# The products of the quantised x with its block scales, walked elements-first instead of blocks-first

## What is computed

```python
def fp4_quant_dequant(x):
    xb = x.reshape(shape[:-1] + (shape[-1] // BLOCK, BLOCK))      # BLOCK = 16
    scale = jnp.max(jnp.abs(xb), axis=-1, keepdims=True) / 6.0
    scale = jnp.maximum(scale, jnp.float32(1e-12))
    xn = xb / scale
    idx = jnp.searchsorted(_MID, jnp.abs(xn))
    q = _GRID[idx] * jnp.sign(xn) * scale
    return q.reshape(shape)
...
gate = fp4_linear(x, w_gate); y = fp4_linear(x, w_up)             # 256 -> 704
h = jax.nn.silu(gate) * y
return fp4_linear(h, w_down)                                      # 704 -> 256
...
x = x + 0.5 * ffn(layernorm(x))
x = x + attn(layernorm(x))     # scan over 512 tokens, 16 states per channel
x = x + 0.5 * ffn(layernorm(x))
```

## Time and profile before

| what | value |
|---|---|
| median of 3 runs | 3746.4 us (3733.61 to 3751.59) |
| the profiled execution's own time | 3731.64 us |
| its span | 3729.6 us |
| VectorE busy | 3399.4 us, 91% |
| TensorE busy (matmul) | 3292.7 us, 88% |
| ScalarE busy | 2999.9 us, 80% |
| GpSimd busy | 2873.4 us, 77% |
| granted TensorE clock, mean | 0.966 |
| DMA queue of SP | 24.3% of 16 engines' span |

### The profile page before, as it was taken

One profiled execution on the slowest core, in us unless ns is written; L12 is line 12 of the kernel. 1 busy time (PEld: TensorE's weight loads), 2 busy tenths in 40 slices (PEclk: granted clock), 3 DMA queues, 4 the chain that ended last, 5 costly groups with the idle time before them and its releaser, 6 DMA issues. The chain is left out here.

```text
span 3729.6 us, 79626 instructions
## 1 busy us (share of the span) xinstructions
PE 3292.7 (88%) x28716; PEld 2351.3 (63%) x28716; DVE 3399.4 (91%) x5419; ACT 2999.9 (80%) x6314; POOL 2873.4 (77%) x2489
## 2 busy tenths in 40 slices
PE   0589999999998999999999999999999999999984
PEld 0256666666666666666666666666666666666663
DVE  5499999999999999999999999999999999999984
ACT  1388888888888888888888888888888888888872
POOL 2458788788877788787878878788888888888854
PEclk9799999999999999999999999999999999999987
DMA  2112222222222222222222222222222222232212
GB/s 37 25 33 49 52 52 54 58 60 46 59 49 51 54 63 47 55 55 49 55 58 61 45 59 49 54 53 60 50 55 60 49 55 54 58 63 43 53 35 43
DMA packets 583023, 192.07 MB, mean 51 GB/s; under 512 B 544039, under 2 KB 578280, under 8 KB 582632
## 3 DMA queue, kind: packets, MB, share of 16 engines
q1 hardware_dynamic: 582632, 186.98, 24.3%
HBM read 19.16 MB, written 16.78 MB: 10 GB/s over the span
## 5 line engine op out<-in xcount | busy, mean ns | idle before, releaser
L787 DVE TENSOR_TENSOR_SCAN state<-w_ps,decay 128x512 f32<-128x512 f32 x1024 | 1210.6, 1208 | 60.3 <-PE w_ps L1303 56.5
L1229 PE MATMUL gu_ps<-wgu,qxT 128*128 128x352 f16 x6144 | 1032.6, 320 | 101.9 <-ACT gate L1048 51.4
L1303 PE MATMUL w_ps<-bdif,x_parts 128*128 128x129 f16 (+1 forms) x12288 | 850.3, 222 | 96.0 <-DVE state L787 88.5
L1303 PEld LDWEIGHTS w_ps<-bdif,x_parts 128*128 128x128 f16 x12288 | 754.0, 98 | 218.4 <-issue 175.3
L1229 PEld LDWEIGHTS gu_ps<-wgu,qxT 128*128 128x128 f16 x6144 | 577.1, 99 | 480.7 <-ACT gate L1048 65.3
L1115 ACT ACTIVATE decay<-dt,A_sb 128x512 f32<-128x512 f32 x1024 | 686.3, 711 | 71.0 <-DVE state L787 43.6
L797 DVE SCALAR_TENSOR_TENSOR c_state<-state,inv_A,rep_ps 128x512 f32<-128x512 f32 x1024 | 723.1, 738 | 7.7 <-issue 3.5
L495 POOL TENSOR_TENSOR bdif<-dif,B_lo 128x516 f16<-128x516 f16 x512 | 535.9, 1060 | 164.7 <-PE w_ps L1303 164.0
L1243 PE MATMUL dn_ps<-wd,qhT 128*128 128x256 f16 (+1 forms) x4608 | 591.6, 279 | 64.0 <-DMA qhT<-qh 62.5
L1323 PE MATMUL y_ps<-ident,c_state 128*128 128x128 f32 x4352 | 621.5, 279 | 22.7 <-DVE c_state L797 22.7
L1103 ACT ACTIVATE bdif<-dif,B_tok 128x129 f16<-128x129 f16 x2048 | 628.9, 393 | 0.0
(11 more groups left out here) (160 smaller groups left out, 3803.3 us busy)
## 6 DMA issues: line engine op xcount, KB each, us to landing
x_in<-in_L_attn_x SPq DMA_DIRECT2D x32, 512.0 KB, 3.8
x_s<-x_a SPq DMA_DIRECT2D x32, 512.0 KB, 3.8
out<-x_out SPq DMA_DIRECT2D x32, 512.0 KB, 3.2
qhT<-qh SPq DMA_TRANSPOSE x256, 3.7
qxT<-qx SPq DMA_TRANSPOSE x128, 3.1
hid<-in_L_ffn_w_gate SPq DMA_DIRECT2D x1, 704.0 KB
bdif<-in_L_ffn_w_up SPq DMA_DIRECT2D x1, 704.0 KB
val<-in_L_ffn_w_down SPq DMA_DIRECT2D x1, 704.0 KB, 13.1
```

The costliest lines, as they stand in the source:

```text
L787: v.tensor_tensor_scan(state[:, n % 2, gi, :], w_ps[:, gi, :], decay[:, n % 2, gi, :], 0.0, ALU.add, ALU.mult).then_inc(state_ready.sem, 1)
L1229: last = te.matmul(gu_ps[:, m, 0:FH], qxT[:, t // 2, 4 * (t % 2) + xp * G + c], wgu[:, c, wp, a:a + FH], start=begin, stop=end)
L1303: last = te.matmul(w_ps[:, gi, t * P:t * P + wide], x_parts[:, seq % 2, xp, t, gi * P:(gi + 1) * P], bdif[:, n % NB, t, bp, 0:wide], start ...
```

## The change

`parts_x` describes the same elements in another order. x_grid and qx keep their layout in memory (position outer, block inner); the instruction now walks them as [tile, block, position], the position innermost. Both x_grid and qx are then stepped by 16 elements (32 bytes) from one element to the next, and each scale is read 16 times in a row. Number of instructions, their sizes, their types, their waits, and the place in every engine's order are the same.

```diff
-            def by_position(t, nb):
-                return t.rearrange("p (t i b) -> p t i b", i=BLOCK, b=nb)
-
-            def over_positions(t, nb, groups):
-                r = t.rearrange("p (t b) -> p t b", b=nb).unsqueeze(2)
-                return r.broadcast_to([t.shape[0], groups, BLOCK, nb])
+            def over_blocks(t, nb, groups):
+                r = t.rearrange("p (t b) -> p t b", b=nb).unsqueeze(3)
+                return r.broadcast_to([t.shape[0], groups, nb, BLOCK])
...
                 for part, s in ((0, x_scale_hi), (1, x_scale_lo)):
-                    v.tensor_tensor(qx[:, a:b, part, :].rearrange("p t (i b) -> p t i b", b=XB_),
-                                    by_position(x_grid[:, a * DM:b * DM], XB_),
-                                    over_positions(s[:, a * XB_:b * XB_], XB_, TH),
+                    v.tensor_tensor(qx[:, a:b, part, :].rearrange("p t (i b) -> p t b i", b=XB_),
+                                    x_grid[:, a * DM:b * DM].rearrange("p (t i b) -> p t b i", i=BLOCK, b=XB_),
+                                    over_blocks(s[:, a * XB_:b * XB_], XB_, TH),
                                     ALU.mult).then_inc(qx_ready.sem, 1)
```

## The result

The changed kernel takes 4209.2 us in the median (4207.2 to 4211.4, 4 runs), the kernel before beside it 3740.0 us. The ratio is 1.129 (95% interval 1.124 to 1.134): 12.9% slower, 483 us by the ratio, where I had forecast 3910 us and a range up to 3995. The direction was right; the size was 2.7 times the 179 us of my sum.

What follows compares the result with a forecast made beforehand. VectorE was taken to bound the kernel. 256 products at 0.757 us more each add 194 us, 15 hide: 3731.6 + 194 - 15 = 3911, forecast as 3910 us (chance 0.60), range 3790 to 3995.

Steps and rivals of the forecast that it cites:

- What bounds the kernel: VectorE is the fullest engine, 94.7% busy in the steady stretch, against TensorE at 93% and POOL at 81%.
- First price, the half rate: Each of the 256 changed products loses its packed rate: 688 ns in place of 415, 273 ns more.
- Second price, the step: 32-byte steps in each changed product: 323 ns for the write, 161 for the read, giving 1172 ns in all.
- The page's figures: Skill page, 32-bit streams: 1.71 ns a column for a hopping write, 1.98 with both reads too; product about 1.17 us.
- Rival 2: The step costs more, up to 1.5 us a product: 278 us less 20, kernel at 3989 us; chance 0.15.
- rival 1: Changed products at half rate with no price for the step: 70 us less 5, kernel at 3797 us; chance 0.12.
- rival 5: Loop order is turned back on the way to the chip, nothing changes: 3732 us; chance 0.03.
- rival 3: The 194 us replace half of VectorE's idle time, 90 us hidden in its waits: 3836 us; chance 0.07.
- Rival 4: Not slower: at N.qy0, POOL stalls (34 us) and 30 us of waits go, at half rate alone: 3738 us; chance 0.03.
- What hides: Only N.qy1's extra 1.5 us, in VectorE's wait for TensorE at the head of ten iterations: 15 us.
- The transpose of N.qy0: Starts 1.5 us later, covered by 2.4 us before TensorE's first gate and up product; no cost.
- The cost beside it, POOL: VectorE's products and POOL exclude each other: 34 us of stalls stay; holding POOL longer costs nothing, 10 us at range top.

Runs made afterwards that it cites:

- e1: Kernel before, with only the scale read 16 times in a row, x_grid and qx both in order: 3786.7 us, ratio 1.015.
- e3: Kernel before, with the scale read 16 times in a row and x_grid's read stepped by 32 bytes, qx in order: 3955.2 us, ratio 1.062.
- e2: Kernel before, with the scale read 16 times in a row and qx's write stepped by 32 bytes, x_grid in order: 4207.2 us, ratio 1.129.

## Why the prediction was wrong, point by point

- **What bounds the kernel: right.** VectorE's busy time rose by 491 us, its idle time fell from 330 to 316 us, and the span grew by 477. Three doses say the same: busy time of the group up by 57, 200 and 545 us in e1, e3 and e2 gave 56, 229 and 480 us by the ratios (in e2 the products overlap as above, so that VectorE's busy time rose by 491 and not 545).
- **First price, the half rate: right.** 684 ns measured in e1 against 688 in the sum, from L724 and the 4-byte rows.
- **Second price, the step: this is the step that failed.** I took "L944, in full for the write, and with half of it again for the read", 484 ns, and let the bounds end at 1500 ns for the product. The write alone costs 1668 ns over e1 where the sum had 323, and the read adds nothing to it where the sum had 161. L944 was a fair witness for its own kind: 4-byte elements pay 1.05 to 1.08 us here too. But the changed write has elements of 2 bytes, and no row of the trace wrote such an element by itself; I noted the smaller size only as a reason for a lower price. The upper bound was built from reads and writes of 4-byte elements and so could not hold it. Adding a share for the read was wrong as well: the two sides do not add in any of the steps tried.
- **The page's figures**, "Vector Engine (DVE) Microarchitecture Reference" of the Trainium skill, section 5.2, led to the same 1.17 us, because they are for 32-bit streams. Where these runs have 32-bit streams, with one read and the write hopping, they come out lower than its 1.98 ns a column for both reads and the write: (1.07 - 0.69)/512 + 1.03 = 1.77 ns, no more than the write alone.
- **Rival 2 had the right sign of the error and the wrong size.** In place of its 278 us the group of products grew by 544, and VectorE's busy time by 491. Rivals 1 and 5 are out by the product's duration, rival 3 by the idle time, which fell by 14 us and not by 90. Rival 4 is out by e1, which has its condition, the half rate alone: it took 62 us more than the kernel before (56 by the ratio), near the 65 of rival 1's sum, and not the 6 of rival 4's.
- **What hides: near in size, partly by luck.** I let 15 us vanish; idle time fell by 14. The waits at the head of an iteration shrank as I had said, from 56.5 us to 29.9 for L784, and none is over 2.7 us, where ten were over 3. But those 27 us are not all of it: the waits of `hid` for TensorE grew by 16 us (65.7 to 81.6) and for ScalarE by 8. And e3, whose product is the nearest to my 1172 ns (1081 and 1075), hid nothing: VectorE's idle time grew by 17 us, its wait at the same place from 56.5 to 90.7, and the stalls beside POOL from 34 to (169 + 334) x 128 = 64. It lost 229 us where my sum with its product would have 256 x 0.66 - 15 = 154. So with the product's price right, the sum would still have been some 75 us short there. Why the waits grew there and shrank in the changed kernel was not tried.

```profile
DVE state L784 <- PE w_ps L1300: 90.7, 34, 3.8
```

- **The transpose of N.qy0: covered, as forecast.** At 2041 us its two products end 5.96 us after the first one's start, against 3.29 at 1930.4. TensorE still waits for it only twice, 30.8 us where it was 21.5, since TensorE is late by the same delay: it waits 235 us for c_state at L1310 and 155 at L1320, where it waited 14 and 23 before:

```profile
PE rep_ps L1310 <- DVE c_state L794: 235.3, 69, 8.5
PE y_ps L1320 <- DVE c_state L794: 154.5, 30, 7.2
```

- **The cost beside it, POOL: a little short.** The stalls, which I had left as they were, rose from 34 to (137 + 302) x 128 = 56 us, and POOL in turn is held: its L484 takes 3.36 us at 2041 us and its next L495 2.66, where they took 2.13 and 1.23:

```profile
2041.23 3.36 POOL L484 TENSOR_TENSOR x_parts<-s_xh,x_parts 128x1024 f16<-128x1024 f32 x1 [0.80 <-ACT x_parts L1089]
2044.56 2.66 POOL L495 TENSOR_TENSOR bdif<-dif,B_lo 128x516 f16<-128x516 f16 x1
```

- **The sum with the measured price:** start to start, two pairs of products take 4.17 and 4.27 us (starts 2080.04, 2084.21 and, of the next instruction, 2088.48 in the timeline) in place of 0.74 and 0.67, 3.50 more for each. 128 x 3.50 = 448, with 22 for stalls and 14 less idle 456 us, against 477 in the spans. The same sum with the right terms comes within 21 us; about 10 of these are busy time of L721 and L726, 4 and 6 us.

## What to carry to other kernels

Ask of every stepped operand three things apart: does it break the packed rate, is it read or written, and does each write fill whole 4-byte words. 512 results of 2 bytes written one at a time, 32 bytes apart, took 2.3 us in a product on VectorE, where the packed product takes 0.42, and 2.33 us on ScalarE and GpSimd; so turn a layout round on a read or on a 4-byte result, or keep two neighbours together. And a scale that has to be repeated can be stored in pairs instead of being read with a step of zero: that edit made this kernel 1.6% faster than before. When no row shows an operation in its own element size, its price has no upper bound in the trace, and the range should say so.

## What the runs showed of the hardware that I had not expected

- The write of lone 2-byte elements takes 2.30 us for 512 columns on VectorE, 2.33 on ScalarE and 2.33 on GpSimd, where they take 0.69 (with the repeated scale; 0.42 packed), 0.62 and 1.15 in order. A `tensor_scalar` on VectorE takes 1.24 for the same writes, and that two-fold difference is not explained here.
- It depends on the step: 0.73 us at 4 bytes, 1.29 at 8, 2.42 at 16, 2.29 at 32, 2.38 at 64, 2.43 at 128.
- Stepped reads and stepped writes do not add: 1.07 and 1.08 alone, 1.07 together; 1.07 and 2.29 alone, 2.29 together.
- The instruction behind one with such writes starts 0.36 us before its end, where ordinary ones overlap by 0.08, and lasts 0.2 us longer: 2.50 for 2.30, and 0.61 for 0.42 in a packed product.
- TensorE's granted clock fell from 0.98 to 0.92 of full speed in the steady stretch, means between its two levels of 1.2 and 2.4 GHz with most of the time at the upper one, while its busy share fell from 93% to 85%, and its products at L1226 went from 320 to 333 ns in the mean. Since VectorE sets the pace, no run here shows a cost of that.
